# One stage of a four-layer graph kernel: scatter, projection and what follows run eight slots behind the gather instead of nine

## What is computed

```python
def _L3_gnn_ref(H, W_lin, W_val, a, W_out, A0, src, dst):
    bt, n, d = H.shape
    h, dh = a.shape                                   # 4 heads of 32
    Xq = (H @ W_lin.T).reshape(bt, n, h, dh)
    Xv = (H @ W_val.T).reshape(bt, n, h, dh)
    Qs = Xq[:, src]                                   # 256 edges
    Kt = Xq[:, dst]
    e = jnp.einsum('behd,hd->beh', jax.nn.leaky_relu(Qs + Kt, 0.2), a)
    e = e + jnp.log(A0[src, dst] + EPS)[None, :, None]
    e_t = e.transpose(1, 0, 2)
    m = jax.ops.segment_max(e_t, src, num_segments=n)
    ex = jnp.exp(e_t - m[src])
    denom = jax.ops.segment_sum(ex, src, num_segments=n)
    attn = ex / denom[src]
    Vt = Xv[:, dst].transpose(1, 0, 2, 3)
    Y = jax.ops.segment_sum(attn[..., None] * Vt, src, num_segments=n)
    return Y.transpose(1, 0, 2, 3).reshape(bt, n, d) @ W_out.T

x = _layernorm(x + _L2_gnn_ref(x, adj, ...), axis=-1)
x = _layernorm(x + _L3_gnn_ref(x, ..., adj, src, dst), axis=-1)
```

## Time and profile before

| | us |
|---|---|
| median of 3 runs | 1007.44 (1007.18 to 1009.31) |
| the profiled execution | 1006.96 |
| its span, first to last instruction | 1005.2 |
| PE busy | 922.8 (92%) |
| DVE busy | 658.7 (66%) |
| ACT busy | 546.1 (54%) |
| POOL busy | 311.8 (31%) |
| mean granted TensorE clock | 0.981 of full speed |

### The profile page before, as it was taken

How to read it: one execution, slowest core, us unless ns; L and a number is a source line. 1 busy time by engine, 2 the same in 40 slices (tenths; PEclk the granted TensorE clock), 3 DMA queues, 4 the chain that set the end, 5 groups by cost and what they waited for, 6 DMA issues and landing times. The chain is left out here.

```text
span 1005.2 us, 14453 instructions
## 1 busy us (share of the span) xinstructions
PE 922.8 (92%) x5144; PEld 792.2 (79%) x5144; DVE 658.7 (66%) x1627; ACT 546.1 (54%) x1136; POOL 311.8 (31%) x290
## 2 busy tenths in 40 slices
PE   6999997999998999999999999899989987678994
PEld 4689986899997888998889899788778863356773
DVE  6664435445546646665655775698897876778877
ACT  2043224655645565554656464557667647466757
POOL 3011222331233233223323323224333220145663
PEclk9989999999999999999999999999999998889998
DMA  8030011001010100101010010301000000000014
GB/s 225 1 82 2 22 53 74 1 22 42 1 43 2 42 22 1 42 2 43 1 43 22 1 43 1 124 1 62 15 31 22 1 1 0 1 0 1 2 43 126
DMA packets 33994, 31.62 MB, mean 31 GB/s; under 512 B 8450, under 2 KB 28034, under 8 KB 33924
## 3 DMA queue, kind: packets, MB, share of 16 engines
q1 hardware_dynamic: 32900, 30.64, 9.9%
q10 hardware_dynamic: 960, 0.07, 0.1%
q0 software_dynamic: 64, 0.00, 0.0%
HBM read 22.83 MB, written 7.87 MB: 31 GB/s over the span
## 5 line engine op out<-in xcount | busy, mean ns | idle before, releaser
L1322 ACT ACTIVATE gates<-psum,gbias 128x256 f32<-128x256 f32 (+2 forms) x312 | 158.9, 565 | 63.5 <-PE psum L67 58.7
L65 PE MATMUL psum<-LS,WI 128*128 128x256 f32 (+2 forms) x312 | 104.1, 334 | 10.0 <-ACT gates L1322 6.3
L67 PE MATMUL psum<-LS,WI 128*128 128x256 f32 (+2 forms) x312 | 102.9, 330 | 0.0
L66 PE MATMUL psum<-LS,WI 128*128 128x256 f32 (+2 forms) x312 | 102.8, 330 | 0.0
L72 POOL TENSOR_TENSOR LS<-A,LS 128x512 fp32r<-128x512 f32 (+2 forms) x44 | 48.9, 1112 | 172.2 <-ACT LS L1307 172.1
L72 POOL TENSOR_TENSOR LS<-Hodd,LS 128x512 fp32r<-128x512 f32 (+2 forms) x44 | 48.8, 1109 | 147.5 <-ACT LS L1307 147.5
L72 DVE TENSOR_TENSOR yl<-psum,yh 128x512 fp32r<-128x512 f32 x58 | 39.6, 689 | 65.0 <-ACT yh L1264 44.2
L72 POOL TENSOR_TENSOR XSl<-X,XSh 128x512 fp32r<-128x512 f32 x32 | 42.3, 1324 | 115.8 <-ACT XSh L1259 115.8
L1329 ACT ACTIVATE tc<-cell 128x512 f32<-128x512 f32 (+2 forms) x88 | 45.3, 514 | 57.8 <-DVE cell L1617 33.7
L65 PEld LDWEIGHTS psum<-LS,WI 128*128 128x128 f32 x312 | 59.2, 190 | 19.5 <-POOL LS L72 10.2
L65 PE MATMUL psum<-B2h,LT2h 128*128 128x256 f32 x256 | 72.7, 284 | 1.0 <-DVE X L1435 1.0
(11 more groups left out here) (368 smaller groups left out, 2674.3 us busy)
## 6 DMA issues: line engine op xcount, KB each, us to landing
WI<-lstm_weights SPq DMA_DIRECT2D x14, 512.0 KB, 3.5
WH<-lstm_weights SPq DMA_DIRECT2D x11, 512.0 KB, 4.5
X<-in_x SPq DMA_DIRECT2D x16, 256.0 KB, 5.4
out<-X SPq DMA_DIRECT2D x16, 256.0 KB, 2.3
lstm_weights<-WI SPq DMA_DIRECT2D x4, 512.0 KB, 2.6
lstm_weights<-WH SPq DMA_DIRECT2D x3, 512.0 KB, 2.7
A<-in_adj SPq DMA_DIRECT2D x4, 256.0 KB, 4.5
z_A<-in_adj SPq DMA_DIRECT2D x1, 1024.0 KB, 5.2
```

The costliest lines, as they stand in the source:

```text
L65: pe.matmul(out, lhs[0], rhs[0], start=start, stop=False)
L66: pe.matmul(out, lhs[0], rhs[1], start=False, stop=False)
L67: return pe.matmul(out, lhs[1], rhs[0], start=False, stop=stop)
L1322: act.activation(gates[:, gate, 0:n], sh.psum[:, gate, 0:n], ACT.Tanh if gate == G else ACT.Sigmoid, bias=gbias[:, p_ - 1, gate:gate + 1]) ...
```

## The change

`BEHIND` goes from 9 to 8, so m is one higher in every slot, and S, P, R, s4, v4, p4, sh4 and ap4 of a batch come one slot earlier. The items va, vh and vl are written with an index one lower, so they stay in the slot in which they were. The hand-written `drain()` begins one batch later and is in another order at its start.

```diff
-    AHEAD, BEHIND = 5, 9
+    AHEAD, BEHIND = 5, 8
...
-            if 0 <= m + 1 < NB:
-                items += [("vh", m + 1)]
+            if 0 <= m < NB:
+                items += [("vh", m)]
...
-            if 0 <= m + 1 < NB:
-                items += [("vl", m + 1)]
+            if 0 <= m < NB:
+                items += [("vl", m)]
...
-            if 0 <= m + 2 < NB:
-                items += [("va", m + 2)]
+            if 0 <= m + 1 < NB:
+                items += [("va", m + 1)]
...
-            first = [("vh", 10), ("sc", 3), ("mx", 3), ("df", 3), ("S", 9), ("vl", 10), ("ex", 3), ("va", 11), ("S", 10),
-                     ("R", 7), ("at", 3), ("vh", 11), ("ec", 3), ("vl", 11), ("p4", 1), ("dn", 3), ("va", 12), ("ap4", 3)]
...
+            first = [("vh", 10), ("sc", 3), ("mx", 3), ("df", 3), ("vl", 10), ("ex", 3), ("va", 11), ("S", 10), ("R", 8),
+                     ("at", 3), ("vh", 11), ("ec", 3), ("vl", 11), ("ap4", 5), ("dn", 3), ("va", 12)]
...
```

More of the change, by code:

```diff
@@ L2073, in drain @@
         def drain():
-            first = [("vh", 10), ("sc", 3), ("mx", 3), ("df", 3), ("S", 9), ("vl", 10), ("ex", 3), ("va", 11), ("S", 10),
-                     ("R", 7), ("at", 3), ("vh", 11), ("ec", 3), ("vl", 11), ("p4", 1), ("dn", 3), ("va", 12), ("ap4", 3)]
-            weighted = [("P", 8), ("P", 9), ("s4", 7), ("R", 8), ("sh4", 1), ("ap4", 4), ("vh", 12), ("S", 11), ("R", 9), ("vl", 12),
[4 rows of a table removed]
-            last = [("P", 13), ("ap4", 7), ("S", 15), ("s4", 12), ("v4", 4), ("p4", 4), ("R", 13), ("sh4", 3), ("ap4", 8),
[1 row of a table removed]
+            first = [("vh", 10), ("sc", 3), ("mx", 3), ("df", 3), ("vl", 10), ("ex", 3), ("va", 11), ("S", 10), ("R", 8),
+                     ("at", 3), ("vh", 11), ("ec", 3), ("vl", 11), ("ap4", 5), ("dn", 3), ("va", 12)]
+            weighted = [("P", 9), ("S", 11), ("vh", 12), ("s4", 8), ("R", 9), ("vl", 12), ("va", 13), ("v4", 2), ("P", 10),
[4 rows of a table added]
+            last = [("P", 13), ("ap4", 8), ("S", 15), ("s4", 12), ("v4", 4), ("p4", 4), ("R", 13), ("sh4", 3), ("ap4", 9),
[1 row of a table added]
                     ("R", 15), ("ap4", 10), ("s4", 15), ("v4", 6), ("p4", 6), ("ap4", 11), ("ap4", 12), ("sh4", 5),
```

## The result

| | before | after |
|---|---|---|
| median, us | 1007.31 (1007.14 to 1009.31, 4 runs) | 1021.56 (1018.31 to 1026.46, 4 runs) |
| the profiled execution, us | 1006.96 | 1022.36 |
| its span, us | 1005.2 | 1020.5 |
| mean granted TensorE clock | 0.981 | 0.967 |
| from the start of dn0 to the end of the span, us | 84.6 | 97.3 |

The ratio is 1.0132, 95% interval 1.0091 to 1.0174. The kernel is slower, as forecast, and by more: 14.25 us in the median, where 8.7 were predicted, and the median lies above the range, which ended at 1019.

A forecast was written before the change was run, and what follows sets the result against it. It took VectorE's chain to bound slots 8 to 11, TensorE slots 12 to 15, then a chain round several engines; 2.6 + 0.9 - 0.7 + 2.0 + 1.1 + 1.3 + 1.9 + 1.1 - 1.5 = +8.7 us, 1016.1 us, range 1010 to 1019.

The forecast's parts named there:

- A: Slot 8: TensorE waits at S0 for vl0, which stands behind a root on GpSimd; +2.6 us.
- B: Slots 9 to 11: S3 waits 0 to 0.9 us, taken as 0.9; a 0.66 us wait before dn1 goes, -0.7.
- F: By the end of slot 11 TensorE has done one S and one P more than before; +2.0 us.
- C: Slots 12 to 14: S6 waits for vl6, behind root p4.0 on GpSimd; +1.1 us, 0 if the root overlapped.
- D: Slot 16: S8 reaches its place on TensorE before vl8 is ready; +1.3 us.
- E: Slot 17: S9 waits for evacuation, ap4.2 and vh9 on ScalarE, then vl9 on GpSimd; +1.9 us.
- G: From W15 to aT3: the chain through ScalarE, vl10 and S10 takes 8.5 us instead of 7.4; +1.1 us.
- H: Drain from aT3 to the end of vl15: 11.4 us instead of 12.9; -1.5 us.
- rival (3): TensorE's clock also falls to 1.2 GHz at the new idle at S10, adding 2.5 us: 1018.6 us; chance 20%.
- The estimate of +3.5 us: Weight-load busy time leaves some 5 us spare in slots 12 to 15, absorbing waits; the prediction didn't follow it.
- rival (1): The shorter tail pays and the waits are absent or covered: faster by 2.4 us, 1005.0 us; chance 7%.
- (2): Rival: waits and gains cancel within 0.2% (2 us), time 1007.4 us; chance 8%.

The follow-up runs named there:

- e3: The changed kernel with constant matmuls filling TensorE's waits ahead of S0, S6, S8, S9 and S10; 1014.8 us, ratio 1.0096.
- e14: The changed kernel with the same five waits filled by constant matmuls, run again word for word; 1015.8 us, ratio 1.0079.
- e5: The changed kernel with GpSimd's roots p3 and p4 moved behind the slot's vl; 1015.8 us, ratio 1.0085.
- e6: The changed kernel with ScalarE's ap4 applications moved behind the slot's vh, one slot later (one batch later in the drain); 1012.4 us, ratio 1.0052.
- e15: The changed kernel unaltered, measured a third time; 1020.8 us, ratio 1.0126.
- e1: The changed kernel unaltered, measured again; 1018.7 us, ratio 1.0133.
- e2: The kernel before, order untouched, with TensorE waiting one slot earlier for each low part of batches 0 to 9; 1014.7 us, ratio 1.0071.
- e11: The kernel before with constant matmuls ahead of its waits in the drain; 1006.2 us, ratio 0.9993.
- e10: e7 with constant matmuls ahead of the waits it has left; 1009.7 us, ratio 1.0031.
- e7: The changed kernel with both GpSimd's roots behind vl and ScalarE's ap4 behind vh; 1011.7 us, ratio 1.0051.
- e12: The changed kernel with constant matmuls only ahead of S8, S9 and S10; 1016.0 us, ratio 1.0079.
- e13: The changed kernel with constant matmuls only ahead of S0 and S6; 1018.4 us, ratio 1.0103.
- e4: The changed kernel with each S(n) issued on TensorE behind W, dn and P of its slot; 1017.0 us, ratio 1.0120.
- e9: e7 with each S(n) of slots 8 to 14 also issued behind W, dn and P; 1014.8 us, ratio 1.0069.
- e8: The kernel before with only its drain reordered: p4.1 behind va12, vh12 ahead of P8, ap4 one batch later; 1007.5 us, ratio 1.0006.

## Why the prediction was too low

At full clock the sum holds: +8.7 predicted, +8.4 in e3, +8.3 in e14. By its steps:

- **A**, S0 waits 2.6 us: 2.55, and G12 starts 949.85 - 943.55 - 2.57 = 3.7 us later in the stretch (4 forecast). e5 shows that the root's place is one microsecond of the wait, and that this microsecond isn't won by dn1 when the root moves.
- **B**, S3 waits 0 to 0.9, taken as 0.9: it waited 0.07. DVE's lateness was absorbed. The step that I chose by "the nearest places were held" was at its low end; together with the vanished 0.66 us wait this is 0.8 us too much.
- **F**, +2.0: by dn1 the loss is 3.7, which is 2.55 + 0.07 - 0.66 + 2.0 less 0.2.
- **C**, S6 +1.1: 1.25, with a root that took 3.28 us instead of 3.01; from dn1 to dn2 the loss is 1.6. In e5 it is gone.
- **D**, S8 +1.3: 1.01. **E**, S9 +1.9: 1.71, and in e6, with ap4 behind vh, 1.21.
- **G**: the idle at S10, forecast at about 3.4, is 3.24 in e15, and 2.49 in after, where the half-speed S9 and P ate the rest. aT3 is 9.6 us later in e3; A to G make 10.2.
- **H**, aT3 to vl15: 11.4 forecast, 11.5 in e3 and 12.7 in before (start to start), a gain of 1.1 where 1.5 were counted (the five terms of the prediction add up to 11.5, not 11.4). After vl15: 0 forecast, and 14.8 to 14.9 us in before, after and e3 alike.

That 8.4 comes so near to 8.7 is in part luck: A, B and F together were 1.0 us too much (4.8 against 3.8 at dn1), C 0.4 and H 0.4 too little.

The step that failed is the clock: the sum has no term for it, and rival (3), which has, was given 20% and 2.5 us. It happened in all three profiled executions of the change, at a price of 2.7 to 5.0 us. Near 2.5 it was only where the clock fell behind S10 (2.7 in e15, 2.2 in the drain of e1). In e1 it fell at S0 as well, which cost 2.8 us more, and for which the prediction names the idle but has no price. In after it fell already behind the waits of S8 and S9 (1.01 and 1.71 us), so that S9, W and P8 ran at half speed too, and the price was 4.3. The argument against it, "slots before it are full", is no argument: the waits at S8 and S9 come ahead of S10 and are two of the new ones. The price should have been counted from the first of the new waits, not from S10. With 8.4 + 4.3 on before's 1007.3 one has 1020; the rest up to 1021.6 is within the spread of the runs (1018.3 to 1026.5), and part of it can be the clock of earlier stages, which the profiled execution shows as 2.6 us ahead of dn0. The range's upper end, 1019, left no room for that spread; its lower end, 1010, doesn't follow from its own +4.5, which gives 1011.9, or 1011.4 with half of G.

The estimate of +3.5 us, by which the weight loads' share left a quarter of slots 12 to 15 spare, was rightly put aside: the slot of after is 957.84 - 952.58 = 5.26 us long against 5.27, and no wait vanished in it. The Trainium skill (TensorE: Matmul & The Clock Gate, section Part 1) calls the slow clock the default that activity lifts. The traces agree in that the clock fell at the waits of S8 to S10 and not where they were filled; e2, where it held through three waits, and e11, where it fell with hardly one, show that this isn't the whole of it.

Rivals (1) and (2) are excluded by all three measurements of the change, whose intervals begin at 1.009. What rival (1) counts on, a tail that pays, is there with 1.1 us in e3 and 2.2 in e10, where it had 4.4; the waits that it holds to be absent are not.

## What to carry to other kernels

A consumer moved one slot nearer to its producer turns slack into waits on an in-order engine: list for each slot what stands ahead of the producer's last step on its own engine (here a root on GpSimd and a block of applications on ScalarE), because that, and not the distance in slots, is the wait. Then add the new idle of TensorE per stretch and price the clock as likely wherever the chain runs over TensorE next; a kernel with a few constant matmuls in the waits shows in its profile what is wait and what is clock. A wait that is made shorter is not yet time won: at S0 one microsecond less of it came back as a wait of 0.75 us at S1, and dn1 was no earlier. A shorter drain is worth little when its chain goes round three engines: one batch less in it paid 1.1 us in e3 and 2.2 in e10.

## What was not expected of the hardware

- The same kernel loses the clock at different places: after S0's 2.56 us wait in e1 and not in after or e15; behind S9 in after, behind S10 in e15. The ends differ by 2.3 us for that, and the time of a run goes with its mean clock: e7's ten runs are 1009.43 at 0.981 and 1015.04 and 1015.16 at 0.969.
- The clock came back to 2.4 GHz in after at 984 us, when PE had worked without a gap since S9 at 980.47, and fell again at 987.4, behind a wait of 2.49 us, for S10 to S12. In e11 it fell with PE hardly idle. What decides it in the drain stays open. Of the moved kernels it was kept in four of four profiled executions with those waits filled (e3, e14, e12, e10) and lost in nine of nine with waits left there (after, e1, e15, e13, e4, e5, e6, e7, e9); with the order of before it was kept in two (before, e2) and lost in two (e8, e11).
- The root p4.0 (128x16) took 3.28 us in after and 3.01 in before, and the one of 12 columns 2.38 against 2.27: a step whose own duration moves by a tenth, in front of a value for which TensorE waits.
